# Opening of the next item as the last part of the search's stream; layer 3's last steps beside the first pairs; two norms' scales folded into weights

## What is computed

```python
def layer0(xn):      # s: gated linear attention; g: coupling net, 3 cycles
    q, k = l2norm(xn @ Wq), l2norm(xn @ Wk); v = xn @ Wv
    beta = sigmoid(xn @ Wbeta)
    for t: state = state * (1 - beta*k*k') + beta*v*k'; out[t] = state @ q[t]
    s = (layernorm(out) * ln_g + ln_b) * silu(xn @ Wg) @ Wout
def layer1(xn):      # s: 2 time mixes; g: 2 blocks of local attention and FFN
    n = norm(h) * ln_w + ln_b; k, v, r = n @ Wk, n @ Wv, sigmoid(n @ Wr)
    h = h + (r * scan(0.95, k * v)) @ Wo
    n = norm(f) * lg + lb; f = f + ((n @ w1a + b1a) * gelu(n @ w1g + b1g)) @ w2 + b2
def layer2(xn):      # s: state-space scan, 16 states; g: 4 experts, best 2
def layer3(xn):      # s: 16 heads: a * (softmax kept to its 25 largest) @ v
                     #    + (1-a) * linear attention; g: coupling net
```

## Time and profile before

| what | us |
|---|---|
| median of 3 runs | 5306.54 |
| lowest and highest of them | 5289.95, 5325.58 |
| the profiled execution, its own time | 5293.35 |
| span of that execution, first to last instruction | 5291.6 |

### The profile page before, as it was taken

The page is one execution under the profiler, slowest core; times in us unless marked ns, Lnnn a source line. Parts: engine busy times, 40 slices in busy tenths (PEclk is TensorE's granted clock), DMA queues, the critical chain, the costliest instruction groups (busy, mean ns, idle before and its releaser), DMA issues. The chain is left out here.

```text
span 5291.6 us, 58321 instructions
## 1 busy us (share of the span) xinstructions
PE 4047.1 (76%) x16660; PEld 1871.0 (35%) x16660; DVE 3994.3 (75%) x7871; ACT 2963.8 (56%) x5740; POOL 2507.6 (47%) x2324
## 2 busy tenths in 40 slices
PE   5776878868877788877888687886887778877676
PEld 1332244423443234422444234442344323443233
DVE  3325688967889678885888778886778867888698
ACT  3443566645666456655566566664566645666443
POOL 1214255544556355562554535544455534556365
PEclk8876898868988788878888699876888777887555
DMA  1000000000000000000000000000000000000000
GB/s 80 1 24 2 2 1 25 1 3 3 1 25 1 3 3 1 25 0 3 3 1 25 3 2 1 25 1 3 3 1 25 1 3 3 1 25 1 2 1 3
DMA packets 7995, 44.07 MB, mean 8 GB/s; under 512 B 848, under 2 KB 848, under 8 KB 7248
## 3 DMA queue, kind: packets, MB, share of 16 engines
q1 hardware_dynamic: 7632, 39.89, 2.0%
HBM read 37.52 MB, written 2.36 MB: 8 GB/s over the span
## 5 line engine op out<-in xcount | busy, mean ns | idle before, releaser
L2032 DVE MAX8 m<-top 128x8 f32<-128x512 f32 x2048 | 1288.4, 678 | 0.2
L2094 POOL TENSOR_SCALAR top<-top,m 128x512 f32<-128x512 f32 x512 | 810.0, 1582 | 965.8 <-DVE m L2032 837.6
L2036 DVE MATCH_REPLACE8 top<-m,top 128x512 f32<-128x512 f32 x1536 | 1026.0, 675 | 0.3
L289 PE MATMUL bank<-arena,consts 128*128 128x512 f32 (+1 forms) x912 | 621.3, 773 | 82.7 <-POOL arena L1644 37.0
L2100 POOL TENSOR_TENSOR top<-top 128x512 f32<-128x512 f32 x512 | 651.4, 1272 | 15.0
L289 PE MATMUL bank<-arena,weights 128*128 128x512 f32 (+8 forms) x976 | 552.2, 686 | 58.3 <-DVE arena L1224 29.5
L1901 PE MATMUL bank<-consts,top 128*128 128x128 f32 x2048 | 401.0, 329 | 208.7 <-POOL top L2100 154.7
L289 PE MATMUL bank<-arena 128*64 128x128 f32 (+3 forms) x3200 | 479.5, 377 | 41.4 <-ACT arena L1085 41.0
L1980 ACT ACTIVATE top<-bank 128x512 f32<-128x512 f32 x512 | 305.3, 596 | 295.2 <-PE bank L1901 294.9
L1901 PEld LDWEIGHTS bank<-consts,top 128*128 128x128 f32 x2048 | 290.7, 169 | 478.0 <-POOL top L2100 314.9
L289 PE MATMUL bank<-top,vt 128*9 128x128 f32 x4096 | 340.8, 321 | 135.8 <-ACT top L1980 135.8
(11 more groups left out here) (293 smaller groups left out, 6468.1 us busy)
## 6 DMA issues: line engine op xcount, KB each, us to landing
arena<-experts_dram SPq DMA_DIRECT2D x32, 768.0 KB, 6.8
weights<-weights_dram SPq DMA_DIRECT2D x1, 6982.0 KB, 19.2
hold<-x_dram SPq DMA_DIRECT2D x9, 256.0 KB, 2.7
out_dram<-x_out SPq DMA_DIRECT2D x9, 256.0 KB, 3.2
consts<-consts_dram SPq DMA_DIRECT2D x1, 1759.5 KB, 23.6
rot<-consts_dram SPq DMA_DIRECT2D x1, 1024.0 KB, 25.6
```

Source lines behind the costliest of these rows:

```text
L289: return nc.tensor.matmul(o, lhsT, rhs, start=start, stop=stop)
L2032: nc.vector.max(m8[:, slot(p, e), k], src).then_inc(SB["top"], 1)
L2036: nc.vector.match_replace(wk_[e], m8[:, slot(p, e), k], sc[slot(p, e)] if k == 0 else wk_[e], -3e38).then_inc(SB["rest"], 1)
L2094: nc.gpsimd.tensor_scalar(pp[e], sc[slot(p, e)], m8[:, slot(p, e), TOPK // 8, 0:1], None, ALU.is_ge).then_inc(SB["kept"], 1)
```

## The change

Four things.

The opening is no part of layer 0 any more. `b_pe` and its sisters append the opening of item b+1 behind the search's steps, so that its 8 steps stand in stream b's tail, beside layer 2's state loop. It uses the search's banks (`O = [X[1], Y, P, X[0]]`) and its tiles `sc`, `ex` and `wk_`, once the search is through with them; DVE's first instruction of it also waits until layer 2 no longer needs the tile that `xn0` shares. In the first block stream b is `SEARCH_STEPS` empty steps and then the opening. The first item's opening (`lead`) gets a block of its own ahead of `run(0, True, False)`, with a barrier behind it. Layer 2's gate and last product move to other tiles, since the opening now writes where they were.

Layer 3 takes 5 of its 11 own steps (and 5 of the coupling's 18) ahead of the search, and the other 6 beside its first steps (`beside`, `at`). The first search pair needs the key and query masks only; the linear attention's results are waited for by the third pair's scores on PE and by GpSimd's first mask.

In the time mix and the FFN of layer 1 the norm's gain is multiplied into the weights in the setup, and its shift becomes a bias: `mix_bias` for k, v and r, added to `b1a` and `b1g` for the FFN. The norm is then one DVE product. In layer 0 the norm's gain and the gate are applied ahead of the root (`Norm.dve`), and the shift goes through Wout by a second matmul of a tile that GpSimd computes from the gate (`sgb`).

The string `SEARCH` has other digits and 192 of them, for 200 before.

```diff
-SEARCH = ("0000100201010030021112113101013222312310616122002111002021101011112002002502113221005112311121015201"
...
+SEARCH = ("0202010232210111100211012062131131120231722100022100302012113i100b0023232100321132321003100101012011"
...
+                    for i in range(DEPTH):
+                        for n, name in enumerate(("Wk", "Wv", "Wr")):
+                            mm(A[1][:, DEPTH * n + i:DEPTH * n + i + 1], W(f"l1_{name}{i}"), W(f"l1_ln_b{i}"))
+                        for n, (o, w) in enumerate(HCH):
+                            at = 8 + 6 * i + 2 * n
+                            mm(A[1][0:w, at:at + 1], W(f"l1_w1_{i}", lo=o, n=w), W(f"l1_lb{i}"))
+                            r = mm(A[1][0:w, at + 1:at + 2], W(f"l1_w1_{i}", lo=HID + o, n=w), W(f"l1_lb{i}"))
+                    r.then_inc(S["shifts"], 1)
...
+                    v.wait_ge(*S("shifts", 1))
+                    for n, share in enumerate((0.5 * (1.0 - 0.95), 1.0, 0.5)):
+                        ts(mix_bias[:, n], A[1][:, DEPTH * n:DEPTH * n + DEPTH], share, None, ALU.mult)
...
+                                at, b = 8 + 6 * i + 2 * n + part, W(f"l1_{name}{n}_{i}")
+                                tt(b, b, A[1][0:w, at:at + 1], ALU.add)
+                        for name, gain in (("Wk", "ln_w"), ("Wv", "ln_w"), ("Wr", "ln_w"), ("w1_", "lg")):
+                            ts(W(f"l1_{name}{i}"), W(f"l1_{name}{i}"), W(f"l1_{gain}{i}"), None, ALU.mult)
...
+                if self.gain is not None:
+                    v.wait_ge(*S(n + "_sq", 1))
+                    stt(self.dst, self.xc, self.gain, self.scale, ALU.mult, ALU.mult).then_inc(S[n + "_g"], 1)
+                    v.wait_ge(*S(n + "_g", 1))
...
-                if self.gain is None:
-                    tt(self.dst, self.xc, self.rs, ALU.mult).then_inc(S[n], 1)
-                else:
-                    stt(self.dst, self.xc, self.gain, self.rs, ALU.mult, ALU.mult).then_inc(S[n + "_g"], 1)
-                    v.wait_ge(*S(n + "_g", 1))
...
+                tt(self.dst, self.xc if self.gain is None else self.dst, self.rs, ALU.mult).then_inc(S[n], 1)
...
+                self.sq, self.rs, self.ksq, self.qsq, self.rk, self.rq, self.beta = *sc, *ex, wk_[0]
+
+            def pe(self, pe, item, search):
                 S = self.S
-                mm(A[0], C("centre"), x0).then_inc(S["op_xc"], 1)
+                if item:
+                    pe.wait_ge(SD.sem["x0"], 16)
+                if search:
+                    pe.wait_ge(*SB("sc", 2 * NP))
+                    pe.wait_ge(*SB("of", 1))
+                    pe.wait_ge(*SB("took", NT))
+                mm(O[0], C("centre"), x0).then_inc(S["op_xc"], 1)
...
-                yield
-                mm(A[0], W("l0_Wk"), xn0).then_inc(S["op_k"], 1)
-                mm(A[1], W("l0_Wq"), xn0).then_inc(S["op_q"], 1)
...
+            def dve(self, v, item):
                 S = self.S
                 yield
                 yield
+                if item:
+                    v.wait_ge(*S2("du", 1))
                 v.wait_ge(*S("op_rs", 1))
...
 
         Layer0 = Layer0()
...
             mm(A[1], W("l0_Wv"), xn0).then_inc(S["v"], 1)
             yield "hop"
             for n in range(18):
...
+            pe.wait_ge(*S("shifted", 1))
+            mm(A[2], W("l0_Wout"), L.sgb, True, False)
             pe.wait_ge(*S("on", 1))
-            mm(A[2], W("l0_Wout"), L.og).then_inc(S["s"], 1)
...
+            nc.gpsimd.tensor_scalar(L.sgb, sg, W("l0_ln_b"), None, ALU.mult).then_inc(S["shifted"], 1)
...
-                act(L.k_sb, A[3], ACT.Copy, scale=0.5 * (1.0 - 0.95)).then_inc(S["k_sb"], 1)
+                act(L.k_sb, A[3], ACT.Identity, scale=0.5 * (1.0 - 0.95), bias=mix_bias[:, 0, i:i + 1]).then_inc(S["k_sb"], 1)
...
-                ts(L.nrm, L.nrm, W(f"l1_ln_b{i}"), None, ALU.add).then_inc(S["mix"], 1)
+                tt(L.nrm, A[2], L.rs, ALU.mult).then_inc(S["mix"], 1)
...
-                tt(A[2], A[2], L.k_sb, ALU.mult).then_inc(S["kv"], 1)
+                stt(A[2], A[2], mix_bias[:, 1, i:i + 1], L.k_sb, ALU.add, ALU.mult).then_inc(S["kv"], 1)
...
+                L.sq, L.rs = sc[0:2]
+                L.qk, L.qk2 = (top[:, T * o:T * o + 2 * T].rearrange("p (a q c) -> p a q c", a=2, q=NT) for o in (6, 10))
+                L.cp = Coupling(S3, "L3", 1, xn_b[:], P, [th_b[:], og_t, og, og_t, og, og_t], small)
+                L.mx, L.qft = ex[0][:, 0:NT * 2 * H3], pp[1]
+                L.carve = Carve(8 * T, 9 * T, top)
+                L.kvm = L.carve(H3 * 9).rearrange("p (h d) -> p h d", d=9)
+                L.mu, L.var = (L.carve(NT * 2 * H3) for _ in range(2))
...
-        BEFORE = 11
...
+        OWN, BEFORE = 11, 5
+        SEARCH_STEPS = 3 + BEFORE + 7 * (NP + 2) + 4
...
+        def beside(steps, mine, cp, last=None):
...
+            at = [*range(0, 8, 2), *range(7, 3 + left)]
             for n, _ in enumerate(steps):
-                if n % 2 == 0 and n // 2 < left:
+                if n in at:
+                    if n in at[:OWN - BEFORE]:
+                        next(mine)
                     next(cp)
-                if last and n == 2 * left:
+                if last and n == at[-1] + 1:
                     last()
...
-                pe.wait_ge(*S("mask", 4))
+                pe.wait_ge(*SB("sc", 3))
...
-                pe.wait_ge(*S("kf", 1))
+                pe.wait_ge(*SB("sc", 4))
...
+                    pe.wait_ge(*S3("mask", 4))
+                if p == 2:
+                    pe.wait_ge(*S3("qft", 1))
                     pe.wait_ge(*S3("ol_a", 2))
...
-            yield
-            yield
             fetch(0, 0)
             fetch(0, 1)
+            yield
...
+                if p == 0:
+                    g.wait_ge(*S3("ol", 1))
...
-            cp = Layer3.cp.dve(v)
-            yield from l3_dve(v, cp)
-            yield from beside(search_dve(v), cp)
-
-        def b_pool(g):
-            cp = Layer3.cp.pool(g)
-            yield from l3_pool(g, cp)
-            yield from beside(search_pool(g), cp)
...
+        now[0] = None
+        with nc.Block(no_gpsimd_drain=True) as block:
+            @block.tensor
+            def _(pe):
+                weave(lead.pe(pe, False, False), None)
...
+        lead_marks.settle()
+        clear(top_marks.sems.values())
         run(0, True, False)
...
```

175 lines of the change are left out of this document (97 added, 78 removed).

## The result

The changed kernel takes 5235.78 us (median of 4 runs, 5231.68 to 5247.88), the kernel before 5304.94 in the same series: ratio 0.9868, interval 0.9836 to 0.9901, so it is faster by about 1.3%. The forecast was 5220, in a range of 5135 to 5310. The profiled execution has a span of 5229.9 us, 61.7 less than before.

The account below looks back on a forecast made before the run. No engine was full; DVE's waits, 130 us an item, were what a change could take. Terms summed to -12.3 us an item, -86 for seven, +8 outside: -78, so 5215 or 5228; forecast 5220, range 5135 to 5310.

Parts of the forecast that it names:

- five figures named as signs of being right: x to layer 0's product 12 us, item 617, DVE busy 495, L1606 waiting 10 to 14, last search's first MAX8 31.
- The fifth: In the state loop, L1606 (L1632 after the change) would wait 10 to 14 us an item.
- The opening leaves the front: Ahead of layer 0, the opening's first matmul to Wv's goes from the path: -18.75 us an item; barrier's 8 us stay.
- State loop: Layer 2's state loop: DVE work moved in +3.5, inserted matmuls on PE +2.5; +6 us an item, bounds 1 and 15.
- End: Item's end: Wk and Wq delay the last gathering, `head8` the output, at 1.2 GHz; +1 us an item.
- Norms: Norms of layers 0 and 1: DVE loses four additions, -3.45 us an item, bounds nothing and 6.
- What is late next: Layer 0, now first behind the barrier, pays for extra matmuls and PE's slow clock: +7 us an item, bounds 0 and 12.
- first pairs: Layer 0: search work moved ahead of its new x fills waits, -4.1 us an item, bounds 0 and -8.
- Once in the run: Outside the seven items: lead's barrier +4, first block +6, setup +7, last search -9; sum +8 us.
- the waits are filled: Rival: extra matmuls keep PE from idling, the tail's granted clock rises; -24 us an item, about 5130 us; chance 0.20.
- It comes back: Rival: PE rules layer 0, its stretch grows by 12, the states by 10; -1 us an item, about 5295; chance 0.20.
- The state loop becomes PE's: Rival: nothing inserted in the state loop is hidden at 1.2 GHz; +13 us an item, about 5400 us; chance 0.07.

Follow-up runs that it names:

- the aligned digits: Changed kernel with the digits of before, search at the same step as before the change in layers 1 and 2: 5130.90 us, ratio 0.9699.

## Why the prediction was right or wrong

The direction, the size (61.7 us in the profiles for 78 forecast) and the range held. That the sum came so near is in part luck: several terms were wrong in opposite ways, and the two largest mistakes, both of more than 10 us an item, cancel.

Of the five figures named as signs of being right, four held: 12.2 us from the end of x to layer 0's first product, 619.2 us an item, DVE busy 498 us an item, 29.4 us to the last search's first MAX8. (The 25 us that the forecast set against the first is the stretch to `kn`; to the product it was 28.7.) The fifth did not: L1632 waits 7.8 us an item for PE, not 10 to 14.

*The opening leaves the front*, -18.75: the stage shows -18.6, and the run with the opening behind x gives 17.2 net of what it costs in its new place. Right, and the costs in the new place were put too high, since 10 to 15 net were expected.

*State loop*, +6: 5.5. Right in sum, wrong in its parts. I let a third of the 8.5 us of waits for PE take up DVE work, of 6.2 us, and added 2.5 for matmuls at 1.2 GHz. The waits stayed (9.6 and 9.7 us) and DVE's work grew by 5.3, so nothing was covered; and without the opening the loop is as long, so its matmuls cost nothing. L2080, an output, takes 1.71 us there, as the sharing of SBUF interfaces told in the Trainium skill (GPSIMD Engine Reference, Specifications) would have it: it starts inside GpSimd's product L1670, which ends at 1088.41, and ends at 1088.44. Over the whole run its median is 0.176.

*End*, +1: -2.4. Wrong. I had laid `head8` and the last gathering at 1.2 GHz onto the path. The last gathering is of the fast kind,

```profile
1135.85 1.12 PE L290 MATMUL bank<-arena,consts 128*128 128x512 f32 x2 [1.51 <-POOL arena L1670]
```

and `kn`, `qn`, `u` do fit into the wait. The step that failed is the choice between the two clocks, -2 or +4.

*Norms*, -3.45: undoing them in layer 1 costs 4.4 us by the profile, 3 by the ratios. Right.

*What is late next* (+7) and *first pairs* (-4.1): layer 0's stage ends at -0.3, with 4.1 us more search in it, but neither term had its size. With the own steps all first, layer 0 takes 15.6 us more than in the changed kernel, and as much more than before the change (104.9 for 89.6). So layer 0 with the opening gone from its front would have lost up to some 15 us, and putting the search's first pairs between the own steps gave it back. I had priced the pairs at the search work that moves; what they seem to do is let layer 0's matmuls go ahead of layer 3's. That wait for PE shows (25.8 us for 10.8), which of the matmuls ahead makes it is argued.

*The digits*: no term at all, and +13.1 us an item. It is one of the two largest mistakes of the sum; it hid behind a second part of the change that I undervalued by about as much. I had read the string as "how much search stands where" and looked at its front and end only.

*Once in the run*, +8: +5.7 (first block +1.8, last search +3.9), right only in sum. The setup is +7.05, as said:

```profile
33.45 2.05 PE L289 MATMUL bank<-hold,consts 128*128 128x512 f32 x2 [4.63 <-PEq L319]
...
52.03 2.05 PE L289 MATMUL bank<-hold,weights 128*128 128x512 f32 x2 [4.03 <-DVE hold L645]
```

before, the opening's first matmul and Wv's; after:

```profile
40.50 2.04 PE L290 MATMUL bank<-hold,consts 128*128 128x512 f32 x2 [4.82 <-PEq L320]
...
61.43 2.04 PE L290 MATMUL bank<-hold,weights 128*128 128x512 f32 x2 [6.61 <-PEq L320]
```

The lead's barrier costs 2.1 us (DVE's wait behind `u`) for 4. The rest of the first block, from Wv on, is 7.6 us shorter (467.3 for 474.9), where I had +6 for its next opening. That opening is free: the block's new x is done at 524.4 us, and at 526.9 in the run that puts it behind x. The shorter norms save some 4; about 3.5 stay unexplained, and the last section shows that this block moves by more between executions of one order. The last search was to gain 9 and lost 3.9. The first MAX8 came 29.4 us behind the first matmul, near the 31 forecast, but

```profile
4863.28 2.07 PE L290 MATMUL bank<-x,consts 128*128 128x512 f32 x2 [5.79 <-PEq L320]
...
4892.71 1.29 DVE L2063 MAX8 m<-top 128x8 f32<-128x512 f32 x2 [5.92 <-ACT top L1997]
...
4911.69 0.82 DVE L1875 COPY ol<-bank 128x288 f32<-128x288 f32 x2 [5.75 <-PE bank L290]
```

DVE waits 5.9 us for the first scores and 5.75 at L1875 for PE, with the second pair's instructions behind it. The failed step: I took the earlier start of the pairs for an earlier end, and left out that own steps in between hold up what is queued behind them.

Of the rivals, "the waits are filled" named 5130 us, which the aligned digits give (5131, at a granted clock of 0.83 instead of 0.81), but not by its mechanism: it had the gain in the tail, where loop and end take 81.7 us for 81.9 in the changed kernel, and the runs have it in layers 1 and 2. "It comes back" wanted 12 us more in layer 0; that shows only with the own steps first. "The state loop becomes PE's" shows up only when matmuls leave their places.

## What to carry to other kernels

An order written out by hand that weaves a periodic stream (here seven steps a pair on four engines) with another can fit one alignment and hardly any beside it: after any change to the number of steps ahead of it, count the stream's instructions at a few landmarks in the old and the new order before pricing anything, for one step cost 6 to 10% of an item here (644.0 and 666.8 us for 605.4). Price a moved piece by what it lets go ahead or holds up on the in-order engines, not by its own length; and read DVE's waits stage by stage with the amount of filler work beside them, since a gain in one stage may be filler taken from another.

## What the runs showed that I had not expected

Some instructions that the change leaves alone take longer on DVE. The product ahead of the state loop (L1599, now L1625) takes 1.36 us before and 2.20 after, those that scale layer 1's queries and keys (L1183, now L1208) a median of 0.68 and 0.85 (ns, least/median/most), before:

```profile
L1599 DVE TENSOR_TENSOR arena<-arena x8: 1226/1356/1358, 442.3 to 4844.3; 128x1024 f32<-128x1024 f32 x8
```

```profile
L1183 DVE SCALAR_TENSOR_TENSOR arena<-arena x64: 666/680/1683, 151.5 to 4613.1; 128x512 f32<-128x512 f32 x64
```

and after:

```profile
L1625 DVE TENSOR_TENSOR arena<-arena x8: 1227/2196/2198, 445.9 to 4774.3; 128x1024 f32<-128x1024 f32 x8
```

```profile
L1208 DVE SCALAR_TENSOR_TENSOR arena<-arena x64: 670/854/1681, 158.5 to 4574.7; 128x512 f32<-128x512 f32 x64
```

Over an item these two lines give back 2.3 us (2.2 for 1.4, and eight of the latter 7.4 for 5.9) of the 3.9 that the norms' lines take off DVE (6.2 for 10.1); that GpSimd is the cause was not tried by a run, but the changed kernel's trace speaks for it. Of the 64 L1208, the 31 that start while GpSimd is in a product of two tensors (L1314 or L2132) take 0.85 to 1.68 us, 28 of the 33 others 0.67 to 0.69 and the last five 0.92 or 0.93; of the eight L1625, the seven that start inside L2132 take 2.20 us and the one beside no GpSimd instruction 1.23.

The first block, with the same order of instructions in both, took 528.1 us in the second profile of the changed kernel and 540.5 in the run with the aligned digits. The columns are those of the earlier trace rows; the granted clock is the third number from the end:

```profile
61.00:500.00 439.00, 324.89 (x1060) 144.22 (x1061) 176.71 (x258) 192.22 (x375) 102.58 (x87) 0.81 0.02 8
```

```profile
61.00:500.00 439.00, 328.72 (x1044) 146.98 (x1045) 165.22 (x248) 184.76 (x363) 91.92 (x81) 0.78 0.02 8
```

DVE, ScalarE and GpSimd are as busy in both up to the block's new x (within 0.2 us); PE is busy 375.0 us for 360.5. So a granted clock of 0.78 instead of 0.81 goes with 12 us here, and what the first block gains or loses by a few microseconds can't be read from one profile.
